# Where SyncE issues the norm rows' transfer in the odd turns of scans 1 to 3

## The reference, cut to what matters

```
Bm = rmsnorm((x @ WB.T).reshape(B, L, H, N), Bn_w) + B_bias
Cm = rmsnorm((x @ WC.T).reshape(B, L, H, N), Cn_w) + C_bias
theta_cumsum = cumsum((x @ Wth.T).reshape(B, L, H, N // 2) * dt[..., None], axis=1)
Bm, Cm = rope(Bm, theta_cumsum), rope(Cm, theta_cumsum)
h_t = alpha_t * h_(t-1) + beta_t * B_(t-1) x_(t-1) + gamma_t * B_t x_t
y_t = C_t h_t
```

## Time and profile before

| what | value |
|---|---|
| median of 3 runs | 3395.3 us (3392.41 to 3405.55) |
| the profiled execution's own time | 3382.4 us |
| its span in the profile | 3380.6 us |
| PE, DVE, ACT, POOL busy | 83%, 69%, 54%, 44% of the span |
| TensorE clock granted in the turns of scans 1 to 3 | 1.00 of full speed |
| turns of scan 1, 2 and 3, from the first score matmul | about 1251 to 1703, 1850 to 2327, 2397 to 2858 us |

### The profile page before, as it was taken

The page is one execution under the profiler, slowest core; times in us unless marked ns, Lnnn a source line. Parts: engine busy times, 40 slices in busy tenths (PEclk is TensorE's granted clock), DMA queues, the critical chain, the costliest instruction groups (busy, mean ns, idle before and its releaser), DMA issues.

```text
span 3380.6 us, 83925 instructions
## 1 busy us (share of the span) xinstructions
PE 2799.0 (83%) x28752; PEld 2118.0 (63%) x28752; DVE 2326.1 (69%) x3926; ACT 1816.0 (54%) x3740; POOL 1501.2 (44%) x1354
## 2 busy tenths in 40 slices
PE   4229997789999789999977999998899998549990
PEld 3118885466666557777754677776577776438870
DVE  5205354789999479999855999994799997324364
ACT  1006654577777167666514777763677774126650
POOL 2470155344444344455500666662456665340256
PEclk7559998899999799999978999999999999669995
DMA  9737896556665255566404666652566662548893
GB/s 389 239 131 233 261 296 200 169 181 198 209 192 179 91 158 156 166 172 173 114 1 127 184 175 169 177 152 63 173 179 182 178 174 77 216 138 256 281 288 118
DMA packets 315367, 609.71 MB, mean 180 GB/s; under 512 B 59152, under 2 KB 163728, under 8 KB 314128
## 3 DMA queue, kind: packets, MB, share of 16 engines
q1 hardware_dynamic: 272352, 501.29, 49.3%
q0 software_dynamic: 24576, 67.14, 6.2%
q10 hardware_dynamic: 18224, 38.54, 3.0%
HBM read 446.25 MB, written 159.51 MB: 179 GB/s over the span
## 4 chain that ended last, share of the span: by engine, by line
PE 63%; DVE 8%; ACT 7%; issue 7%; another core or an unknown queue 6%; DMA 5%; POOL 2%; ACTq 1%; SPq 1%; DVEq 0%; POOLq 0%
PE bank L64 23%; PE bank L572 6%; PE bank L1220 6%; PE bank L1350 4%; PE bank L1414 3%; PE bank L1390 3%; PE bank L1416 3%; PE bank L563 2%; PE cs_sn L586 2%; ACT btr L1365 2%; PE bank L1359 2%; PE bank L586 2%; DMA xl<-xd 1%; ACT sq L1231 1%
## 5 line engine op out<-in xcount | busy, mean ns | idle before, releaser
L64 PE MATMUL bank<-xh,wb 128*128 128x512 f32 x2048 | 677.7, 412 | 71.4 <-ACT btr L1365 37.8
L64 PEld LDWEIGHTS bank<-xh,wb 128*128 128x128 f32 x2048 | 367.6, 189 | 188.6 <-ACT btr L1365 58.1
L1229 ACT ACTIVATE xbc<-bank,norm_w 128x512 f32<-128x512 f32 x512 | 350.7, 685 | 234.0 <-PE bank L64 227.5
L1306 POOL TENSOR_TENSOR rot<-rot,tmp 128x512 f32<-128x512 f32 x256 | 330.7, 1292 | 204.0 <-DVE tmp L1298 204.0
L64 PE MATMUL bank<-xl,wb 128*128 128x512 f32 x1024 | 406.6, 397 | 0.0
L572 PE MATMUL bank<-wgu,xgT 128*128 (+1 forms) x1536 | 327.2, 337 | 92.0 <-issue 71.9
L648 DVE TENSOR_TENSOR hh<-sg,bank 128x96 f32<-128x96 f32 x384 | 97.5, 254 | 408.7 <-ACT sg L622 212.8
L1318 POOL TENSOR_TENSOR sq<-cst,rho 128x512 f32<-128x512 f32 x128 | 133.6, 1044 | 494.7 <-DVE xbc L1274 275.1
L1307 POOL TENSOR_TENSOR rot<-rot,tmp 128x512 f32<-128x512 f32 x256 | 331.4, 1295 | 0.0
L1298 DVE SCALAR_TENSOR_TENSOR rot<-xbc,bias,cs_sn 128x1024 f32<-128x1024 f32 x256 | 325.4, 1271 | 8.6 <-DVE xbc L1274 6.8
L1298 DVE SCALAR_TENSOR_TENSOR tmp<-xbc,bias,cs_sn 128x1024 f32<-128x1024 f32 x256 | 326.1, 1274 | 0.0
(11 more groups left out here) (293 smaller groups left out, 5840.3 us busy)
## 6 DMA issues: line engine op xcount, KB each, us to landing
wb<-watt_dram SPq DMA_DIRECT2D x96, 1024.0 KB
rr_bc<-rr_dram SPq DMA_DIRECT2D x128, 512.0 KB, 6.5
yd<-ys SPq DMA_DIRECT2D x96, 512.0 KB
wd<-w_down SPq DMA_DIRECT2D x384, 96.0 KB
dt_bc<-row_dram SPq DMA_DIRECT2D x256, 128.0 KB
al_bc<-row_dram SPq DMA_DIRECT2D x256, 128.0 KB
watt_dram<-wb ACTq DMA_DIRECT2D x29, 1024.0 KB, 5.2
xd<-xg SPq DMA_DIRECT2D x12, 2048.0 KB, 23.8
```

The source lines that it names most:

```text
L64: ins = e.matmul(dst, a, m, start=start and c == 0, stop=stop and c == n - 1, skip_group_check=not (start and stop))
L1229: e.activation(xbc[j % 4][:, i, :], of(i)[:, :], ACT.Copy, scale=norm_w[:, i:i + 1])
L1306: e.tensor_tensor(R[:, 2 * ty, :], R[:, 2 * ty, :], tmp[:, 2 * ty + 1, :], ALU.subtract)
```

## The change

In `turn_sp` the call of `R_rows` moves from behind the two weight loads of the turn (`th_load_sp`, `wb_load_sp`) to ahead of them. Nothing else is changed. The condition is the same as before: odd turns of scans 1 to 3, without the last one of a scan.

```diff
@@ -1582,6 +1582,8 @@
                     e.wait_ge(e_H.sem, e_H.at(n - 1))
                     e.nop(nofuse=True)
                     end_sp(e, q + 2, j + 2)
+                if RG and not is_first(b):
+                    R_rows(e, gm + 1)
                 if not (last and j >= 1):
                     e.wait_ge(e_th.sem, e_th.at(n + 2))
                     e.nop(nofuse=True)
@@ -1591,8 +1593,6 @@
                     e.nop(nofuse=True)
                     if not is_first(b):
                         wb_load_sp(e, b, q + 4, j)
-                if RG and not is_first(b):
-                    R_rows(e, gm + 1)
                 if not (last and j >= 2):
                     e.wait_ge(e_D.sem, e_D.at(n + 1))
                     e.nop(nofuse=True)
```

## The result

| what | before | after |
|---|---|---|
| median of 3 runs | 3395.3 us (3392.41 to 3405.55) | 3444.63 us (3442.78 to 3453.99) |
| the profiled execution's own time | 3382.4 us | 3442.78 us |
| its span | 3380.6 us | 3441.0 us |

The changed kernel is slower: ratio 1.0145, 95% interval 1.0102 to 1.0189. The medians differ by 49.3 us and the two profiled executions by 60.4; the interval of the ratio, +35 to +64 us, holds both. The forecast was +42, 3437 us, with a range of 3392 to 3480.

What follows compares the result with a forecast made beforehand. PE bounds a 28.9 us pair; the change makes the root-to-root loop the bound, 17.1+12.9 = 30.0. At 1.05 us over 42 pairs, 44 less 2.6 gives about +42 us: 3437 us, range 3392 to 3480.

Steps and rivals of the forecast that it cites:

- What goes: In odd turns of scans 1 to 3, all DVE waits for `rc_in` go, worth 2.6 us and no more.
- What moves: SyncE issues `wb` at R+2.04 instead of R-3.2 (R: end of ACT's root); the later weights are not missed and cost nothing.
- What is late next: `rr_dram`, now behind `wb`, lands 8.0 us after `wb`'s issue, so `rr_bc` is issued at R+10.0 instead of R+6.6.
- the rule that the prediction weighed: A semaphore's increment lands after every earlier write of its DMA engine; `rr_dram` would wait for `wb`'s and `al_bc`'s slowest share.
- From there to DVE: From `rr_bc`'s issue to the even turn's multiply 7.1 us, so the multiply starts at R+17.1 against R+15.3.
- The sum: Over three scans, 42 affected groups of norms at 1.05 us give 44, less 2.6: about +42 us, 3437 us.
- Rival C: The queue is worse: 9.7 us to landing, multiply at R+18.9, 2.9 us over, 42 times: +120, 3515 us; chance 0.1.
- What slack there is: The loop root, `rr_bc`, multiply, root has 2 us slack; it bounds a pair once root to multiply exceeds 16.0 us.
- Rival A: The queue holds `rr_dram` too little: landing within 6.9 us of `wb`'s issue, multiply by R+16.0, 3392 us; chance 0.26.
- Rival B: DVE is the hidden bound of the scans; removing its waits pays about 20 us, giving 3375 us; chance 0.02.
- Rival D: The change does nothing, as SyncE might reach the loads after the root anyway; chance under 0.01, counted with A.
- The signs named beforehand: No `rc_in` wait, `wb` 2 us after root, `rr_dram` to `rr_bc` 4 to 6 us, L1274 waiting, 30 us pairs, PE idle.

Runs made afterwards that it cites:

- only `th` behind the rows: Against the kernel before, odd turns issue `wb`, `rc_in`, `th`, `al_bc`, `rr_dram`, `rr_bc`, so only the `th` load follows the rows; ratio 0.9997.
- chain-ahead run: Against the kernel before, odd turns issue `rc_in`, `al_bc`, `rr_dram` and `rr_bc` all ahead of `th` and `wb`; 3502.08 us, ratio 1.0350.
- Both runs that used ACT's queue: ACT issues `rr_dram` in the changed kernel: 3454.48 us, ratio 1.0195; ACT issues `rc_in` in the kernel before: 3397.35 us, ratio 1.0038.
- half and quarter of `wb`: The changed kernel with the odd turns' `wb` load cut to its first half, ratio 1.0001, or first quarter, ratio 0.9988, against the kernel before.
- `th` last: The changed kernel with odd turns ordered `rc_in`, `wb`, `al_bc`, `rr_dram`, `rr_bc`, `th`; ratio 1.0012 against the kernel before.
- the wait alone: The order of before, but SyncE waits for the root ahead of the weight loads, the rows staying behind them; 3639.43 us, ratio 1.0752.

## Why the prediction was right

The forecast was the loop, and each term can be set beside what the changed kernel shows, as means over the same 41 odd turns:

| term | forecast | measured |
|---|---|---|
| `wb` issued | R+2.04 | R+2.10 |
| from there to `rr_bc`'s issue | 8.0 | 7.96 |
| `rr_bc`'s issue to the multiply | 7.1 | 7.53 |
| root to multiply | 17.1 | 17.60 |
| multiply to next root | 12.9 | 12.85 |
| a pair more than before | 1.05 | 1.47 |
| 42 pairs, less the waits that go | +42 | +60.3 in the profiled pairs, +49.3 in medians |

- **What goes**: right. The `rc_in` waits vanish in the turns, and the version with only `th` behind the rows puts the gain of that at nothing measurable, in line with 2.6 us.
- **What moves**: right that the weights are not missed. The chain-ahead run shows how near that is: at R+8.7 PE waits 99.3 us for `wb` in all.
- **What is late next**: right in kind. That the mean, 7.96, meets the 8.0 so closely is in part luck: in the 18 turns whose multiply comes before R+17 it is 7.1, in the 15 after R+18 it is 9.0, and only seven of the 41 lie within 0.3 us of 8.0. The step that failed in it is the reason, as far as "the small transfer behind `wb`" is read as order in SyncE's queue. Both runs that used ACT's queue show that a queue of its own does not spare the write the wait, so it is for something that the two queues share, the DMA engines. For this change it made no difference to the number; it would have, had someone tried to mend the change that way. Of the rule that the prediction weighed, one half came true: the write waits for the slowest share of `wb`. But the sum did not come to lie at its high end.
- **From there to DVE**: the term that was mis-sized. I took 7.1 us; it measured 7.53, and both rows that I had, 7.22 and 8.5, were longer. The Trainium skill (DMA: Bandwidth & Descriptors, section on the anatomy of one DMA), by whose figures I had estimated 4.4 us for the two `rr_bc`, is as far off here as in the kernel before, and the measurement decides; that section gives its figures for transfers that GpSimd issues, and these are SyncE's. 0.43 us by 42 is 18 us, which is all of the gap between +42 and the profiled +60.3.
- **The sum**: its 1.05 us a pair is a little below what its own terms give, 17.1+12.9-28.9 = 1.1, by which it would be +44. It also stands for a mean that few pairs have. The 18 early pairs take 0.5 us more than before each, the 15 late ones 2.7, so these 15 hold 41 of the 60 us. Rival C, R+18.9, is not the mean, but it is what these 15 pairs show; my forecast treated it as an outside case.
- **What slack there is**: right. The point of about 16.0 us is between 15.83, with no loss, and 16.74, the pair shown above, which took 29.59 us from root to root.
- **Rival A** (no change) fell: the landing takes 7.96 us, not 6.9. Three of the experiments (half and quarter of `wb`, `th` last) have what rival A wanted, a multiply by R+16.0, and they show no loss, so its condition was the right one. **Rival B** fell: with only `th` behind the rows all `rc_in` waits of the turns are gone and nothing else is late, and the time did not move. **Rival D** fell with the timeline.
- **The signs named beforehand**: all appeared, the wait of L1274, the gap of `rr_dram` to `rr_bc` (5.8 us in the mean), pairs of about 30 us, PE idle for L1365 (49.8 us, where it was 37.8). PE also idles 48.5 us for L1399, where it was 35.3, which I had not named; L1399 follows the late rotation, so it is the same loop seen from the outputs' side.

That some landings take 5 us and others 7, with the same issues ahead of them, comes from the last share of `wb`, as the packets above show. Not settled is what makes that share late; no run here varies it.

## What to carry to other kernels

Before moving a wait ahead of a large transfer, ask which small transfer will then stand behind it, and whether that one is on a loop. Write the loop's length down next to the bound's: a lateness is free up to the difference and is paid once per round beyond it, and here half of `wb`, or 0.9 us and 256 KB, decided between no loss and 1.5%. A large load has a window, and here its best place was in front of the wait that it does not need; another issuing queue did not get a small transfer past it. And look at how a landing is spread before putting one number on it: what counts is when the last share of the large load is through, which here varied by 3.5 us.

## What the runs showed of the hardware

- A 16 KB write issued while 1.25 MB of loads are under way is seen landed 4.2 to 7.3 us after its issue, and 1.6 us after it when nothing is. It follows the last packet of the load, which ends between R+6.5 and R+10.0. Issued on the other queue it is no sooner: 6.3 us in the mean, up to 7.7, against 5.8 and 7.3.
- With 512 KB less in front the landing comes 1.83 us sooner, with 768 KB less 2.72.
- **The clock.** The changed kernel's turns have PE busy for 25.8 us longer with the same work, at a granted clock of 0.98 instead of 1.00. In the even turn of the long pair the timeline has PE waiting for DVE, and the stretches of 2 us have its clock behind that:

```profile
2241.21 0.23 PE L1414 MATMUL bank<-x1p,sq 128*64 128x16 f32 x1 [1.68 <-DVE st L1399]
```

```profile
2238.00:2240.00 2.00, 1.53 (x8) 0.23 (x4) 2.00 (x3) 0.32 (x1) 1.91 (x2) 1.00 0.41 95
2240.00:2242.00 2.00, 0.79 (x26) 0.79 (x28) 1.92 (x5) 1.21 (x2) 2.00 (x3) 0.99 0.00 0
2242.00:2244.00 2.00, 2.00 (x33) 1.96 (x32) 2.00 (x2) 0.81 (x2) 1.06 (x1) 0.50 0.11 32
2244.00:2246.00 2.00, 2.00 (x66) 1.88 (x63) 1.43 (x4) 1.85 (x2) 1.21 (x1) 0.50 0.00 1
```

The even turn's matmuls before it were at 1.00. PE was idle for 1.68 us, and then ran at 0.50 of full speed, 1.2 GHz, for 4 us or more. In the changed kernel this costs nothing of its own: multiply to next root is 12.84 us in this pair and 12.85 in one at full clock, since the loop does not pass over the slowed matmuls. In the run with the wait alone it does pass over them, and the 1.8 us that a pair has beyond the loop's sum go with the lower clock. A wait that is small against PE's work can thus grow by the clock that follows it; in these two kernels it did so only where the loop goes through PE.
